# Attention over paged keys: weight chunks converted in their own low part's place, with new places, times and an earlier spot in the queue

## The reference

```python
x = x + einsum('bsi,boi->bso', x, weight[adapter_ids])        # x: 8 x 128 x 512
q = rope(rmsnorm(x @ Wq.T))      # 32 heads of 128
k = rope(rmsnorm(x @ Wk.T))      #  8 heads of 128
v = x @ Wv.T                     #  8 heads of 128
k_all, v_all = concat(cache[block_table], new)   # 512 cached + 128 new keys
scores = where(valid, q @ k_all * SCALE, -1e30)
x = x + (softmax(scores) @ v_all) @ Wo.T
```

## Time and profile before

| what | us |
|---|---|
| median of 3 runs | 1035.59 |
| lowest and highest of them | 1033.76, 1040.68 |
| the profiled execution, whole | 1041.16 |
| its span in the profile | 1039.4 |
| PE busy, of the span | 1008.6 (97%) |
| DVE, ACT, POOL busy | 856.1, 801.4, 782.5 |

### The profile page before, as it was taken

One profiled execution on the slowest core, in us unless ns is written; L12 is line 12 of the kernel. 1 busy time (PEld: TensorE's weight loads), 2 busy tenths in 40 slices (PEclk: granted clock), 3 DMA queues, 4 the chain that ended last, 5 costly groups with the idle time before them and its releaser, 6 DMA issues.

```text
span 1039.4 us, 19557 instructions
## 1 busy us (share of the span) xinstructions
PE 1008.6 (97%) x5510; PEld 869.6 (84%) x5510; DVE 856.1 (82%) x1779; ACT 801.4 (77%) x2092; POOL 782.5 (75%) x802
## 2 busy tenths in 40 slices
PE   7898999999999999999999999999999999999997
PEld 5676889898888888888888888888888888888885
DVE  6574657676889998998989898988989989898894
ACT  4363546665888898888888988898888878988884
POOL 3775666665588888887888878897878868888672
PEclk9899999999999999999999999999999999999999
DMA  8588889896688888878789897898898988797973
GB/s 269 149 275 291 252 256 234 238 242 162 124 147 171 162 150 166 142 158 162 143 152 172 148 162 154 156 156 161 148 160 156 158 151 163 141 174 132 161 148 66
DMA packets 472125, 179.53 MB, mean 173 GB/s; under 512 B 415042, under 2 KB 452051, under 8 KB 469971
## 3 DMA queue, kind: packets, MB, share of 16 engines
q1 hardware_dynamic: 366384, 148.93, 68.7%
q10 hardware_dynamic: 104610, 27.26, 12.4%
q0 software_dynamic: 1024, 2.10, 0.7%
HBM read 109.25 MB, written 35.66 MB: 139 GB/s over the span
## 4 chain that ended last, share of the span: by engine, by line
PE 79%; SPq 8%; DMA 3%; DVE 3%; issue 3%; ACT 3%; POOL 1%; ACTq 0%; POOLq 0%; DVEq 0%
PE S L1280 18%; PE O L1213 6%; PE O L1215 6%; PE O L1214 6%; PE Q L1215 5%; PE Q L1213 5%; PE Y L1213 5%; PE Q L1214 5%; PE Y L1215 5%; PE Y L1214 5%; PE T L1219 4%; SPq L303 3%; PE KV L1213 2%; PE KV L1214 2%; PE KV L1215 2%
## 5 line engine op out<-in xcount | busy, mean ns | idle before, releaser
L991 DVE SCALAR_TENSOR_TENSOR pr<-pr,rc,raw 128x640 f16<-128x640 f32 x204 | 234.3, 1149 | 20.4 <-ACT raw L751 15.2
L966 DVE CUSTOM_DVE_ANT_0 pr<-S,mask,rst 128x640 f32<-128x640 f32 x256 | 225.3, 880 | 29.6 <-PE S L1280 26.0
L771 ACT ACTIVATE pr<-pr,nb 128x640 f32<-128x640 f32 x256 | 211.6, 827 | 24.8 <-DVE nb L966 24.8
L751 ACT ACTIVATE raw<-pr,rc 128x640 f16<-128x640 f32 x204 | 163.2, 825 | 2.9 <-DVE rc L982 2.7
L561 POOL TENSOR_TENSOR m<-m 128x512 f32<-128x512 f32 x64 | 111.4, 1740 | 68.6 <-DVE m L1019 65.9
L1280 PE MATMUL S<-kh,qh 128*128 128x320 f32 x512 | 121.9, 319 | 9.7 <-DVE nb L966 8.5
L515 POOL TENSOR_TENSOR kl<-raw,kh 128x512 fp32r<-128x512 f32 x64 | 95.9, 1498 | 34.5 <-ACT kh L650 33.4
L536 POOL TENSOR_SCALAR ptl<-first 128x512 fp32r<-128x512 f16 x130 | 102.3, 787 | 24.2 <-DMA first<-pr 14.0
L712 ACT ACTIVATE Q<-Q 128x128 f32<-128x128 f32 x256 | 68.3, 267 | 67.6 <-DVE m L1019 67.6
L1280 PEld LDWEIGHTS S<-kh,qh 128*128 128x128 f32 x512 | 91.5, 189 | 31.3 <-DVE nb L966 10.6
L1280 PE MATMUL S<-kl,qh 128*128 128x320 f32 x512 | 116.4, 309 | 0.6 <-POOL kl L515 0.6
(11 more groups left out here) (141 smaller groups left out, 2716.1 us busy)
## 6 DMA issues: line engine op xcount, KB each, us to landing
cache_rows<-in_kv SPq DMA_DIRECT2D x80, 256.0 KB, 5.0
wraw<-in_wall SPq DMA_DIRECT2D x73, 256.0 KB, 3.2
raw<-cache_rows SPq DMA_DIRECT2D x63, 256.0 KB, 3.2
raw<-cache_rows ACTq DMA_DIRECT2D x49, 256.0 KB, 4.0
cache_rows<-in_kv ACTq DMA_DIRECT2D x48, 256.0 KB
mask<-mask_rows SPq DMA_DIRECT2D x64, 128.0 KB
first<-in_lw SPq DMA_DIRECT2D x6, 1024.0 KB
acc<-in_x SPq DMA_DIRECT2D x8, 256.0 KB
```

Of the source, the lines that this page charges most:

```text
L751: e.activation(upper16[:, g, :], pr[:, slot(u, g), :], ACT.Copy, scale=rc[:, u % 2, g:g + 1]).then_inc(a_f1, 1)
L771: e.activation(pr[:, slot(u, g), :], pr[:, slot(u, g), :], ACT.Exp, bias=nb[:, u % 2, g:g + 1], scale=-1.0, accum_out=sm[:, u % 2, g:g + 1 ...
L966: e.tensor_tensor_reduce(pr[:, slot(u, g), :].rearrange("p (a n) -> p a n", a=2), S[:, :, 0:320], mask[:, u % 2, :].rearrange("p (a n) -> ...
L991: e.scalar_tensor_tensor(out=lower16(u, g), in0=pr[:, slot(u, g), :], scalar=rc[:, u % 2, g:g + 1], in1=upper16[:, g, :], op0=ALU.mult, op ...
```

## The change

- The raw chunk lands where its low part will stand. The low part is formed in place. `wraw` and `wl` are one stretch of 15 places, `wh` has 14: 29 chunks as before. The detours of the first head over `pr` and `turned` go.
- `load_w` waits for the products that last used its place, 15 chunks back, not for a low part 3 chunks back. ACT's split waits for the products 14 chunks back.
- The tables change. Loads: one a period and head but in two periods (now 4 before the head and its own first); before, four periods had two. High parts on ACT: chunks 2 to 5 move. Low parts on POOL: chunk 2 to place 1, chunk 3 to place 0, chunk 4 from place 0 of the period before the head to place 1 of the one before that, chunk 8 from place 0 of period 2 to place 1 of period 1.
- `next_weights` stands right behind `load_mask` from period 6 on; from 12 on that is ahead of `turn_upper(i, 0)`.

```diff
 HI_ACT = {(0, 6): (1, 0), (0, 7): (1, 1), (0, 8): (1, 1), (0, 9): (2, 0),
-          0: (-5, 0), 1: (-4, 0), 2: (-4, 1), 3: (-2, 0), 4: (-2, 1), 5: (-2, 0),
+          0: (-5, 0), 1: (-4, 0), 2: (-3, 0), 3: (-3, 1), 4: (-2, 0), 5: (-2, 1),
           6: (0, 0), 7: (0, 1), 8: (1, 0), 9: (1, 1)}
 LO_DVE = {(0, 6): (1, 1), (0, 7): (1, 1), (0, 9): (2, 1), (1, 4): (-2, 1), (1, 5): (-2, 1)}
-LO_POOL = {(0, 8): (1, 1), 0: (-5, 1), 1: (-4, 1), 2: (-3, 0), 3: (-2, 1), 4: (-1, 0),
-           5: (-1, 0), 6: (0, 1), 7: (1, 0), 8: (2, 0), 9: (2, 0)}
-LOAD_AT = {0: -6, 1: -6, 2: -5, 3: -4, 4: -3, 5: -3, 6: -1, 7: -1, 8: 0, 9: 0}
+LO_POOL = {(0, 8): (1, 1), 0: (-5, 1), 1: (-4, 1), 2: (-3, 1), 3: (-2, 0), 4: (-2, 1),
+           5: (-1, 0), 6: (0, 1), 7: (1, 0), 8: (1, 1), 9: (2, 0)}
+LOAD_AT = {0: -6, 1: -5, 2: -4, 3: -4, 4: -3, 5: -2, 6: -1, 7: 0, 8: 0, 9: 1}
...
-        wh = sb("wh", [P, NWS * WC], F32R)
-        wl = sb("wl", [P, NWS * WC], F32R)
-        wraw = sb("wraw", [P, NWR, WC])
+        wh = sb("wh", [P, NWH * WC], F32R)
+
+        w_at = nc.sbuf_base
+        wraw = sb("wraw", [P, NWL * WC])
+        wl = nc.alloc_sbuf_tensor_at("wl", [P, NWL * WC], F32R, offset=w_at)
...
             def load_w(hk, c):
-                n = NWC * hk + c
-                if n >= NWR and not (hk == 0 and c in BESIDE):
-
-                    old, oc = divmod(RAW_BEFORE.get(n, n - NWR), NWC)
-                    e.wait_ge(w_lo[oc], old + 1)
+                wait_products(e, NWC * hk + c - NWL)
                 e.dma_start(w_raw(hk, c), wall[hk, :, c * WC:(c + 1) * WC]).then_inc(d_w[c], 16)
...
                 if i + 1 < NU:
                     load_mask(i + 1)
+                next_weights(i)
                 if i == NA:
                     load_k(e, i + 2)
...
                     turn_upper(i, 1)
                     turn_lower(i, 1)
-                next_weights(i)
```

More of the change, by code:

```diff
@@ L29 @@
 NWC = 10
-NWS = 13
-NWR = 3
+NWH = 14
+NWL = 15
 N_WARM = 34
@@ L167, in build @@
         inv_s = cst[:, 3:67]
-        side = turned[:, :, :].rearrange("p t n -> p (t n)").bitcast(F32)
-        w_beside = (side[:, 0:WC], pr[:, 2, 0:WC], pr[:, 3, 0:WC], side[:, WC:2 * WC])
         qkw_s = acc[:, NB - 4, 0:2 * D]
@@ L322, in l0_bank, with wh_cols, wl_cols, wait_products @@
             return Y[:, :] if b <= 3 else KV[:, :]
-        def w_cols(hk, c):
-            n = (NWC * hk + c) % NWS
+        def wh_cols(hk, c):
+            n = (NWC * hk + c) % NWH
+            return slice(n * WC, (n + 1) * WC)
+        def wl_cols(hk, c):
+            n = (NWC * hk + c) % NWL
             return slice(n * WC, (n + 1) * WC)
         def w_raw(hk, c):
-            if hk == 0 and c in BESIDE:
-                return w_beside[BESIDE.index(c)]
-            n = NWC * hk + c
-            return wraw[:, RAW_PLACE.get(n, n % NWR), :]
+            return wraw[:, wl_cols(hk, c)]
+        def wait_products(e, n):
+            if n >= 0:
+                old, oc = divmod(n, NWC)
+                u = NB * old + NB - 1
+                if oc < 4:
+                    e.wait_ge(p_q, 4 * u + oc + 1)
+                elif oc < 6:
+                    e.wait_ge(p_kv, u + 1)
+                else:
+                    e.wait_ge(p_y, 4 * u + oc - 6 + 1)
         def x_cols(b):
@@ L460, in _ @@
                     load_mask(i + 1)
+                if i + 2 >= NL:
+                    next_weights(i)
                 if i + 2 < NL:
@@ L471, in _ @@
                     copy_pages(b, t)
-                next_weights(i)
+                if i + 2 < NL:
+                    next_weights(i)
             for i in range(NA, NU + 2):
@@ L519, in split_w @@
                     e.wait_ge(w_hi[c], hk + 1)
-                    minus(wl[:, w_cols(hk, c)], w_raw(hk, c), wh[:, w_cols(hk, c)]
+                    minus(wl[:, wl_cols(hk, c)], w_raw(hk, c), wh[:, wh_cols(hk, c)]
                           ).then_inc(w_lo[c], 1)
@@ L653, in split_chunk @@
                 e.wait_ge(d_w[c], 16 * (hk + 1))
[L654 to L665, removed]
+                wait_products(e, NWC * hk + c - NWH)
+                rounded(wh[:, wh_cols(hk, c)], w_raw(hk, c)).then_inc(w_hi[c], 1)
             def split_w(period, place):
@@ L1257, in project_q @@
                         e.wait_ge(w_lo[t], hk + 1)
-                    three(Q[:, :], xh[:, t, x_cols(b)], xl[:, t, x_cols(b)], wh[:, w_cols(hk, t)],
-                          wl[:, w_cols(hk, t)], t == 0, t == 3).then_inc(p_q, 1)
+                    three(Q[:, :], xh[:, t, x_cols(b)], xl[:, t, x_cols(b)], wh[:, wh_cols(hk, t)],
+                          wl[:, wl_cols(hk, t)], t == 0, t == 3).then_inc(p_q, 1)
             def project_kv(v):
@@ L1268, in project_kv @@
                 for t in range(4):
[L1269 to L1272, removed]
+                    hi = wh_cols(hk, 4 + t // 2).start + t % 2 * 256
+                    lo = wl_cols(hk, 4 + t // 2).start + t % 2 * 256
+                    made = three(KV[:, 0:256], xh[:, t, x_cols(b)], xl[:, t, x_cols(b)],
+                                 wh[:, hi:hi + 256], wl[:, lo:lo + 256], t == 0, t == 3)
                 made.then_inc(p_kv, 1)
@@ L1357, in project_o @@
                 three(y_bank(u), oh[:, r * P:(r + 1) * P], ol[:, r * P:(r + 1) * P],
-                      wh[:, w_cols(hk, 6 + r)], wl[:, w_cols(hk, 6 + r)], r == 0, r == 3
+                      wh[:, wh_cols(hk, 6 + r)], wl[:, wl_cols(hk, 6 + r)], r == 0, r == 3
                       ).then_inc(p_y, 1)
```

3 lines of the change are left out of this document (removed).

## The result

The changed kernel takes 1032.57 us (median of 12 runs, 1026.23 to 1036.88). The kernel before, run beside it 12 times, takes 1040.38 (1033.76 to 1047.81). The ratio is 0.9921, with an interval of 0.9902 to 0.994: 0.8% less, where 0.7% was forecast. In microseconds 1032.57 lies in the range that was given (1023.5 to 1036), 4.1 above the likeliest value (1028.5) and above the band of 1025.5 to 1031.5 that had most of the chance. The 1035.59 ahead of the prediction is the median of three runs that lay low; with twelve, the kernel before is at the 1041.16 of its profiled execution within 0.1%. In the changed kernel all lines stand two to eight off: the marker is L1374, the scores L1278, the transposes L417 and L427, the weight loads L385, POOL's low parts L523, `lower_plane` L989, ACT's split L658.

A forecast was written before the change was run, and what follows sets the result against it. PE's own work (97% busy) bounds the kernel, so only its waits can be won. Profiled: 1041.16 - 6.9 - 3.9 + 0.5 = 1030.9; median: 1035.59 - 6.9 + 0.5 = 1029.2, with 0.7 more 1028.5; range 1023.5 to 1036.

The forecast's parts named there:

- Chunks 4 and 8 leave place 0: POOL's low parts: the six long periods ahead of a head lose their 6.60 us excess; 6.9 with the rest.
- the rule's sum: By the skill's SBUF port-lock rule alone, moving chunks on POOL from place 0 to 1 would gain near 0.
- The 0.3 for chunks 8 and 9: POOL: most of the remaining 0.28 us excess lies where both stand at place 0; parting them gains 0.3.
- Loads behind the mask: SP's queue: weight loads leave the spot ahead of heads 2 and 3's transposes; 3.9 of four bad periods' 5.81 us won.
- Profile and median: Median run, 5.57 us shorter than the profiled one, was taken to have few of the four long periods; 0.7 won there.
- The start: Second head's chunk 1, loaded a period later, costs one more ACT wait: between 0 and 3.56 us, 0.5 taken.
- In place: POOL's low part formed in place takes 1.30 us, as into another place; no cost.
- the wait on products: Loads wait for products 15 chunks back; SP waits some 3 us in period 6, at no cost.
- A: Rival, chance 0.15: both gains count in full in the median run; 1024.8 us, or 1022.9 with the whole 5.81.
- B: Rival, chance 0.15: the POOL collision only moves and makes DVE late elsewhere; 1035.6 us, up to 1036.1.
- C: Rival, chance 0.10: loads at the new spot delay last transposes, up to 1046.5 us, or weights at ACT, 6 us.
- the limit of 4.3 us: Last transpose's landing time above which each us was said to cost PE one us, in two-load periods.

The follow-up runs named there:

- e1: Changed kernel with only the separation on POOL undone (chunk 3 back at place 1, chunk 4 at place 0 ahead of the head); 1037.49 us, ratio 0.9971.
- e8: Changed kernel with only chunk 4's low part moved back to place 0 ahead of the head, beside chunk 5's; 1026.47 us, one run.
- e4: Kernel before with only the weight loads moved behind the key mask from period 12 on, second head's chunk 9 still loaded at 0; 1038.39 us, ratio 0.998.
- e0: The changed kernel run again, nothing altered; 1029.57 us against 1040.14 for the kernel before, ratio 0.9894.
- e3: Changed kernel with the second head's chunks 0 and 1 split half a period later; 1030.99 us, ratio 0.9907.
- e5: Changed kernel with the second head's chunks 0, 1 and 3 loaded, split and lowered about a period later; 1029.7 us, ratio 0.9898.
- e12: The kernel before run once more, unchanged, for the spread of its profile; 1040.34 us.
- e10: Changed kernel with one extra 256 KB transfer behind each weight load from period 13 on, at the new spot; 1048.34 us.
- e6: Kernel before with 66 in place of 34 warming transposes on PE at the start; 1036.17 us.
- e11: Kernel before with one extra 256 KB transfer behind each weight load from period 13 on, at the old spot; 1092.07 us.
- e9: Changed kernel with POOL's `keys_lo` behind `q_sum` in period 13 only; 1032.69 us, ratio 0.9939.

## Why the prediction was right, and where it was off

**Chunks 4 and 8 leave place 0: right for 6.6 of the 6.9.** The first profile shows the six periods gone; e1 puts 6.18 back by this edit alone, and 5.2 to 7.9 in the medians. The choice against the rule's sum (near 0) was right, and for the reason given: the chunk at place 1 does collide, 1.50 us, with slack behind (a little more than the 1.4 that the prediction allowed there as a sign of being right). e8 adds what the step lacked: three are needed, and in e1 the harm is done through `keys_lo` and the `lower_plane` behind the one that the earlier trace rows show. The 0.3 for chunks 8 and 9 was misread. The one period with them that was long, by 0.36, followed a last transpose at 13.77 after the marker. In the changed kernel, with the chunks apart, the same period is still 0.15 too long, and its transpose landed at 13.64.

**Loads behind the mask: the mechanism right, the size off in both sums.** In the profiled execution the four periods lost all their 5.81, where 3.9 were taken. The 3.9 counted SP's time at one for one. But PE's idle time in the four was 4.13 us in all for 5.81 of period time, at a granted clock of 1.00 throughout: an idle microsecond cost 1.4, and why is not shown. In the median 0.7 were taken and e4 shows 1.8, with an interval from no change to 4.5. The reason given for the smaller number was half right: the part does vary, 5.81, 2.5 and 0 in three profiles of kernels with the old spot (the last with shifted instructions), and is not a fixed term.

**Profile and median: wrong, and the good percentage is partly luck.** I took it that the median run is 5.57 us shorter than the profiled one and has little of the second term. That difference came from three runs that lay low. With 12 runs the median of the kernel before is 0.8 us from its profile. Because I took the second term small for that reason, 1028.5 came out 0.7% below 1035.59; measured is 0.8% below 1040.38. In microseconds the median lost 7.8 where 7.1 were forecast; in e0 10.6. The forecast's own terms for the profiled execution (6.9 + 3.9 - 0.5 = 10.3), set against 1040.38, would have given 1.0%. The baseline, 4.8 too low, is also what put 1028.5 below the measured 1032.57.

**The start: 0.5 taken, 3.3 measured, neither told from chance.** ACT waited 8.71 for a weight, outside the bound of 3.56. But e3 and e5 take the wait away and win nothing, and repeated programs spread over 2.7 us there. As a term of the change it is not told from 0. As a spread of the profiled sum it was missing: 1041.16 - 12.09 + 3.29 + 0.10 = 1032.46 against the 1030.9 forecast (1032.49 is the profiled execution's time).

**In place, and the wait on products: right at nothing.** 1298 ns in place, against 1.30 us in the earlier trace rows. SP did wait for PE's products: 5.20 us in period 6, where some 3 were forecast, and 0.48 to 1.40 us at three loads of the steady part, after which the periods take 14.52 all the same. The wait was not taken away in a run of its own.

**The rivals.** A (both in full, 10.8 us less or more): the profiled execution's steady part behaved so, and e0's median, 10.6 below, is nearer to it than to the forecast. The result's 7.8 is nearer to the forecast's 7.1. B (the collision only moves): false, in the profiles of the changed kernel (the first and e0) no wait for the maximum came up in the steady part. C (loads disturb what lands beside them): its first condition came true. Weights land after 4.6 us for 3.2, and the keys' landing goes with the spot alone: 4.0 to 4.3 in four profiles with the old one, 5.0 to 5.4 in ten with the new. The Trainium skill, "DMA: Bandwidth & Descriptors", section "Queues, rings and completion order", has each engine go round the queues packet by packet; the trace agrees in that both slow down, and shows no more than that. The price stayed out, but not by the limit of 4.3 us that I had estimated: 7 of 50 last transposes took longer than that in the changed kernel, 4.60 at most, and cost 0.2 or less, and in the kernel before it was 6 of 50. What counts is when the transpose lands after the marker (the table under e12), and so its issue as much as its landing. e10 shows that the rival is real with twice the transfers. Its price was too low: each us of wait was taken at one us, but waits of 2.1 us cost 2.9, and 4.4 with a fall of the clock.

## What to carry to other kernels

A collision or a long instruction costs only where the next engine has no slack behind it, so count how many of them stand close together before taking a rule's price. Split a profile's excess into what comes in every execution at the same place and what varies (a second profile of the same kernel showed it here), and take only the first as a sure gain. Take the time to compare with from more than three runs: three lay 4.8 us below twelve. Small transfers in a queue belong where the next transfer waits for something else anyway, and what they slow down there must be looked up in its landing time.

## What the runs showed of the hardware

- A DMA transpose's issue of 1.2 to 1.3 us can take 1.5 to 2.8 when a 16 KB transfer of PE's instructions overlaps it: so it was in all 24 slow issues of e6 and all 16 of the kernel before. Another 10 and 11 met one and stayed fast. Weights in flight go with slow issues too, without such a transfer (14 of 33 in e4).
- A wait of PE of 2.11 us (e11) and one of 2.80 (e10) were followed by a granted clock of 0.50, 1.2 GHz, for some 3 us; equal waits of 2.16 and 2.80 in the same two kernels were not, and their periods are 1.5 us shorter. In the three longest of the four bad periods of the kernel before PE is idle for 1.13 to 1.17 us in all, and the granted clock stays at 1.00.
- The undisturbed period has two lengths. It is 14.52 us in most profiled executions, but 14.46 in e8, e9 and in e10 up to 804 us, which after two long periods runs at 14.52 from 836 us on. Of the 0.06, 0.04 build up over the first 6.4 us after the marker and the rest over the last 4.4, with no idle time of PE in either kernel, so no wait makes them. It is worth 2.9 us in a run; all three kernels are forms of the changed one, but others of that kind do not show it. The cause is open.
- The same extra transfers cost 49 us at one spot in a queue and 19 at another (e11, e10).
